# Five 64-token slots in the expert stage of a fused attention and mixture-of-experts kernel, their second layer with the weights stationary

## The reference

```python
x = x + xattn(layernorm(x), ctx)          # cosine similarity with a context, 256 wide
x = x + attention(layernorm(x))           # 16 heads of 16
x = x + ffn(layernorm(x))
# ffn: 14 experts, each token goes to one
logits = x @ router_w
assignments = argmax(logits); weights = softmax(logits)[assignments]
hid = gelu(x @ w1[e] + b1[e])             # 256 -> 512
out = (hid @ w2[e] + b2[e]) * weights     # 512 -> 256
```

## Time and profile before

| | |
|---|---|
| median of 3 runs | 495.64 us (494.65 to 496.19) |
| the profiled execution | 494.51 us |
| its span, first to last instruction | 492.7 us |
| TensorE busy | 479.8 us, 97% |
| TensorE weight loads busy | 384.0 us, 78% |
| granted TensorE clock | 1.000 |
| VectorE, ScalarE, GpSimd busy | 68%, 67%, 50% |

### The profile page before, as it was taken

One profiled execution on the slowest core, in us unless ns is written; L12 is line 12 of the kernel. 1 busy time (PEld: TensorE's weight loads), 2 busy tenths in 40 slices (PEclk: granted clock), 3 DMA queues, 4 the chain that ended last, 5 costly groups with the idle time before them and its releaser, 6 DMA issues.

```text
span 492.7 us, 13958 instructions
## 1 busy us (share of the span) xinstructions
PE 479.8 (97%) x4290; PEld 384.0 (78%) x4291; DVE 335.6 (68%) x1021; ACT 331.6 (67%) x804; POOL 243.9 (50%) x428
## 2 busy tenths in 40 slices
PE   8999999999999999999999999998999999999996
PEld 6544444567888888888888888877898999999995
DVE  3577665657788989999898999998573333333332
ACT  2765666569988998898898889886553334333432
POOL 3468764344444456474655657472555333233333
PEclk9999999999999999999999999999999999999999
DMA  8989997500001223313322221227465876675631
GB/s 305 284 195 298 297 311 207 177 2 2 1 2 39 51 88 98 98 61 87 100 57 91 67 59 51 67 84 227 152 220 160 266 229 203 207 232 192 193 131 37
DMA packets 35025, 69.32 MB, mean 141 GB/s; under 512 B 6592, under 2 KB 21826, under 8 KB 34960
## 3 DMA queue, kind: packets, MB, share of 16 engines
q1 hardware_dynamic: 31168, 59.40, 40.3%
q0 software_dynamic: 3360, 8.84, 4.8%
q10 hardware_dynamic: 432, 0.26, 0.2%
HBM read 57.61 MB, written 11.35 MB: 140 GB/s over the span
## 4 chain that ended last, share of the span: by engine, by line
PE 65%; DVE 6%; issue 4%; ACT 3%; POOL 2%; POOLq 0%; ACTq 0%; DVEq 0%
PE psum L1532 13%; PE psum L1545 12%; PE psum L1459 9%; PE psum L1436 6%; PE psum L1423 6%; PE psum L1415 6%; PE psum L1383 5%; PE psum L1488 5%; PE psum L1282 5%; DVE arena L912 1%; POOL tok L528 1%; POOL out L614 1%; ACT arena L1145 0%; DVE smax L901 0%; ACT arena L1181 0%
## 5 line engine op out<-in xcount | busy, mean ns | idle before, releaser
L1532 PEld LDWEIGHTS psum<-arena,ring 128*128 128x128 f32 x608 | 73.5, 192 | 2.6 <-issue 0.6
L1532 PE MATMUL psum<-arena,ring 128*128 128x128 f32 x608 | 74.1, 275 | 0.5 <-issue 0.5
L1545 PE MATMUL psum<-w_s,arena 128*128 x304 | 71.9, 380 | 0.0
L1215 ACT ACTIVATE arena<-psum 128x256 f32<-128x256 f32 x38 | 14.6, 385 | 81.7 <-PE psum L1282 74.8
L1036 DVE SCALAR_TENSOR_TENSOR arena<-psum,slot_rec,arena 128x256 f32<-128x256 f32 x38 | 18.4, 484 | 69.3 <-PE psum L1545 69.0
L556 POOL TENSOR_TENSOR ov<-o_n,v_s 128x256 f32<-128x256 f32 x32 | 26.1, 817 | 77.8 <-DVE o_n L794 77.8
L1545 PEld LDWEIGHTS psum<-w_s,arena 128*128 128x128 f32 x304 | 55.0, 190 | 6.1
L1181 ACT ACTIVATE arena<-kT,head_mask 128x256 f32<-128x256 f32 x128 | 59.3, 531 | 0.0
L614 POOL DMA_INDIRECT out<-arena,token_of x38 | 38.8, 1022 | 19.0 <-POOL token_of L606 14.1
L901 DVE TENSOR_REDUCE smax<-psum 128x16 f32<-128x1024 f32 x32 | 39.2, 1224 | 12.6 <-PE psum L1436 12.6
L1145 ACT ACTIVATE arena<-arena 128x1024 f32<-128x1024 f32 x32 | 33.8, 1057 | 19.0 <-DVE arena L912 18.9
(11 more groups left out here) (206 smaller groups left out, 1072.9 us busy)
## 6 DMA issues: line engine op xcount, KB each, us to landing
ring<-w SPq DMA_DIRECT2D x38, 512.0 KB
w_s<-ctxT SPq DMA_DIRECT2D x15, 768.0 KB, 8.5
w_s<-w SPq DMA_DIRECT2D x16, 448.0 KB, 3.4
slot_rec<-routed SPq DMA_DIRECT2D x38, 132.0 KB
tok<-x SPq DMA_DIRECT2D x16, 256.0 KB, 7.8
w_s<-xT SPq DMA_DIRECT2D x12, 256.0 KB, 6.8
routed<-pad_rec SPq DMA_DIRECT2D x1, 1980.0 KB, 8.6
tok<-b SPq DMA_DIRECT2D x14, 128.0 KB, 3.1
```

Of the source, the lines that this page charges most:

```text
L1532: mm = pe.matmul(hid_bank(p)[:, f * P:(f + 1) * P], w1_s[:, r, c * F + f * P:c * F + (f + 1) * P], xgT[:, p, c * P:(c + 1) * P], start=c = ...
L1545: mm = pe.matmul(bank(2 + q, D), hidT[:, q, f * P:(f + 1) * P], w2_s[:, bass.ds(e * (FC * D) + f * D, D)], start=f == 0, stop=f == FC - 1)
```

## The change

`EVEN` becomes 33 full slots, and five *half slots* of 64 tokens are put in at places 22, 25, 28, 31 and 34, so that 38 places are run always as before (`ALWAYS`), and 50 at most (`PLACES`). A half slot serves an expert whose token count leaves 64 or fewer over full slots. The steps are no longer a loop but written out.

In a half slot the records, the normalised tile, the moving operand of the first layer, the gelus and the rows of the output are 64 wide or long. The second layer is turned round: 128x128 blocks of w2 are stationary and 64 columns of the hidden values move, ScalarE copies the result from PSUM (`copy_turned`), and TensorE turns it back with two transposes (`turn_back`) one step later. Its w2 blocks come from DRAM in another order, five more loads of 512 KB by SyncE at slots 12, 14, 16, 18 and 20. The plan gets a second kind of count (`counts[:, 1]`, a subtraction, a maximum), and behind `plan_tables` two new pieces, `plan_halves` and `later_tables`.

```diff
+HALVES, HALF0, APART = 5, 22, 3
-EVEN = NTOK // P + E // 2 - 1
+EVEN = NTOK // P + 1
...
             def plan_counts():
-                plan(dve.tensor_scalar(counts[:, :], count, -1.0, None, ALU.add))
+                for n, short in enumerate((1, 1 + RG)):
+                    plan(dve.tensor_scalar(counts[:, n], count, -float(short), None, ALU.add))
...
+                plan(dve.tensor_tensor(ends[:, 0, 1, PAD0:], ends[:, 0, 1, PAD0:], ends[:, 0, 0, PAD0:], ALU.subtract))
+                settle()
+                at = sums_of(2)
+                plan(dve.scalar_tensor_tensor(ends[:, at, 0, PAD0:], ends[:, at, 1, PAD0:], -float(HALVES),
+                                              ends[:, at, 0, PAD0:], ALU.max, ALU.add))
+                settle()
...
+            def plan_halves(at):
+                plan(dve.scalar_tensor_tensor(half_from[:, 0:E], ends[0:1, at, 0, PAD0:], -float(P), origin[0:1, 0:E],
+                                              ALU.mult, ALU.add))
+                plan(dve.memset(half_from[:, E:E + 1], float(E * REGION - RG)))
+                plan(dve.scalar_tensor_tensor(passed_half[:, :, :],
+                                              ends[0:1, at, 1, PAD0:].unsqueeze(1).broadcast_to([1, HALVES, E]), -1.0,
+                                              slot_row[0:1, 0:HALVES].unsqueeze(2).broadcast_to([1, HALVES, E]),
+                                              ALU.mult, ALU.is_lt))
+                settle()
+                plan(dve.tensor_tensor(half_rise[:, :], half_from[:, 1:E + 1], half_from[:, 0:E], ALU.subtract))
+                plan(dve.tensor_reduce(expert_half[:, :], passed_half[:, :, :], AX.X, ALU.add))
+                settle()
+                plan(dve.tensor_tensor(risen_half[:, :, :], passed_half[:, :, :],
+                                       half_rise[:, :].unsqueeze(1).broadcast_to([1, HALVES, E]), ALU.mult))
+                plan(dve.tensor_scalar(expert_half[:, :], expert_half[:, :], float(E - 1), None, ALU.min))
+                settle()
+                plan(dve.tensor_reduce(base_half[:, :], risen_half[:, :, :], AX.X, ALU.add))
+                settle()
+                plan(dve.tensor_scalar(base_half[:, :], base_half[:, :], half_from[:, 0:1], float(RG), ALU.add, ALU.add))
+                settle()
+            def later_tables():
+                for n, (table, of_half) in enumerate(((expert_tab, expert_half), (base_tab, base_half))):
+                    spread = table[:, HALF0:HALF0 + APART * HALVES].rearrange("o (h r) -> o h r", r=APART)
+                    between = (APART - 1) * HALVES
+                    at = n * P + HALF0
+                    dve.tensor_copy(spread[:, :, 0], of_half[:, :]).then_inc(s["halves_ok"], 1)
+                    dve.tensor_copy(spread[:, :, 1:], bank(7)[0:1, at:at + between].rearrange("o (h r) -> o h r", r=APART - 1))\
+                        .then_inc(s["halves_ok"], 1)
+                    dve.tensor_copy(table[:, HALF0 + APART * HALVES:], bank(7)[0:1, at + between:n * P + NSLOT])\
+                        .then_inc(s["halves_ok"], 1)
...
             finish_slot(5, 5)
             plan_tables()
+            plan_halves(at)
+            later_tables()
...
+                if i == HEAD + 1:
+                    sp.wait_ge(s["halves_ok"], HALVES_TOLD)
+                n, odd = divmod(i - HEAD - 1, 2)
+                if 0 <= n < HALVES and not odd:
+                    of_half = sp.value_load(expert_tab[0:1, bass.ds(HALF0 + APART * n, 1)], min_val=0, max_val=E - 1)
+                    sp.dma_start(w2_half[:, n, :], w2e[bass.ds(of_half, 1)].rearrange("o p j -> (o p) j"))\
+                        .then_inc(s["w2_half_in"], 16)
...
+            def second_layer_turned(u, q):
...
+                for d in range(KC):
+                    for f in range(FC):
+                        mm = pe.matmul(bank(6)[:, d * RG:(d + 1) * RG], w2_half[:, n, f * D + d * P:f * D + (d + 1) * P],
+                                       hidT[:, q, f * P:f * P + RG], start=f == 0, stop=f == FC - 1)
...
+            def turn_back(u, q):
+                pe.wait_ge(s["g_yT"], halves_before(u) + 1)
+                need(pe, s["g_y"], u - 1)
+                turn(bank(2 + q, D), yT[:, :, :].rearrange("p d j -> p (d j)"), s["g_y_psum"])
...
-                t, u = i + 1, i - 1
+                t, u, v = i + 1, i - 1, i - 2
...
                 if within(i, part):
                     first_layer(i, k % 4)
+                if half(v):
+                    turn_back(v, (k - 2) % 2)
                 if within(t, part):
                     turn_slot(t, (k + 1) % 2)
+                if half(u):
+                    second_layer_turned(u, (k - 1) % 2)
+                elif within(u, part):
                     second_layer(u, (k - 1) % 2, e)
```

More of the change, by code:

```diff
@@ L35 @@
 NSLOT = NTOK // P + E - 1
-EVEN = NTOK // P + E // 2 - 1
+EVEN = NTOK // P + 1
+HALVES, HALF0, APART = 5, 22, 3
+HALVES_TOLD = 6
+ALWAYS = EVEN + HALVES
+PLACES = NSLOT + HALVES
 REGION = NTOK + P
@@ L55 @@
 RECS = 8
-LOOPED = HEAD + 1 + (EVEN - HEAD - 2) // RECS * RECS
 LOG_SCALE = 2.0 ** -10
@@ L97, in run_slots, with half, halves_before, width @@
 def run_slots(engine, step, first, last, used_tab, begin=0):
-    run_steps(engine, lambda i, k: step(i, k, (0, EVEN)), begin, EVEN + last, HEAD + 1, LOOPED, RECS)
+    for i in range(begin, ALWAYS + last):
+        step(i, i % RECS, (0, ALWAYS))
     used = engine.value_load(used_tab[0:1, 0:1], min_val=0, max_val=NSLOT)
     with engine.If(used > EVEN):
-        for i in range(EVEN + first, NSLOT + last):
-            step(i, i % RECS, (EVEN, NSLOT))
+        for i in range(ALWAYS + first, PLACES + last):
+            step(i, i % RECS, (ALWAYS, PLACES))
+def half(t):
+    return HALF0 <= t < HALF0 + APART * HALVES and (t - HALF0) % APART == 0
+def halves_before(t):
+    return sum(half(n) for n in range(t))
+def width(t):
+    return RG if half(t) else P
 def within(t, part):
@@ L1077, in _ @@
             plan_tables()
+            plan_halves(at)
+            later_tables()
             def expert_step(i, k, part):
-                t, u = i + 1, i - 1
+                t, u, v = i + 1, i - 1, i - 2
                 if within(t, part):
                     normalise_slot(t, (k + 1) % RECS)
-                if within(u, part):
+                if half(v):
+                    finish_slot(v, (k - 2) % RECS)
+                if within(u, part) and not half(u):
                     finish_slot(u, (k - 1) % RECS)
@@ L1261, in expert_step @@
                     act.wait_ge(s["plan_ok"], 3)
+                if i == HALF0:
+                    act.wait_ge(s["halves_ok"], HALVES_TOLD)
                 if within(i, part):
                     e = expert_of(i)
+                if half(i - 2):
+                    copy_turned(i - 2)
                 if within(t, part):
```

143 lines of the change are left out of this document (88 added, 55 removed).

## The result

The changed kernel takes 500.66 us (500.09 to 502.43, four runs) against 495.91 us of the kernel before. The ratio is 1.0097, with a 95% interval of 1.0066 to 1.0127. A second comparison, in the experiments, gave 1.0086 (1.0062 to 1.0111), +4.3 us. The change makes the kernel slower by 0.9%.

The account below looks back on a forecast made before the run. TensorE was taken to bound the expert stage, with VectorE's plan on the path between slots 5 and 7. Half slots +0.75, plan +0.6 and +1.8 made +3.15 us, 498.8 us on the median; range 495.8 to 501.0.

Parts of the forecast that it names:

- the prediction's own case: Whole kernel: half slots and both plan parts add +3.15 us, bounds 497.7 to 500.0 us; chance 0.60.
- The floor of a pair: TensorE, half slots: a pair with 128 weight columns costs what its load costs, 0.1075 us at 64 moving columns.
- The rival in which the moving columns set the pace: TensorE, half slots: 64 columns cost half, the change is -5.1 us, 490.5 us; chance 0.14.
- A half slot: TensorE: layers -0.06 and -0.01, `turn_back` +0.22, so +0.15 us each and +0.75 in five.
- The plan, part one: VectorE's list ahead of L1012: more instructions in `plan_counts`, TensorE already waiting, +0.6 us (0.5 to 0.7).
- The plan, part two: VectorE ahead of `normalise_slot(8)`: 2.2 us of new list, TensorE stands once for 1.8 us (1.3 to 2.3).
- the rival's paragraph: VectorE at slot 8: part two of the plan hidden or far cheaper, change +0 to +1.4 us; chance 0.16.
- No wait in the half slots: Half slots: ScalarE's copy of the turned result has 1.2 us of cover; narrower work on waiting engines saves nothing.
- The transfers: SyncE's queue, slots 12 to 21: five 512 KB loads stay covered at 276 GB/s on average, costed at 0.
- The rival of late transfers: Slots 12 to 21: w1 or records late, TensorE waits 1 to 2 us at two or three, about 503; chance 0.10.
- Writing the loop out: Expert loop: costs nothing, since steps ahead of the loop and inside it average 3.75 us.

Follow-up runs that it names:

- A second comparison: The changed kernel run once more with no edit, against the kernel before: 500.02 us, ratio 1.0086 (1.0062 to 1.0111).
- the 16-column run: Changed kernel with 16 instead of 64 moving columns in both layers of the half slots, 48 of 64 tokens left out: 499.93 us in one run.
- the narrower weights: Changed kernel with each half-slot weight block given as two of 64 columns: 495.51 us with the halves alternating, 501.57 us with the lower half first.
- Putting slot 8 first: Changed kernel with the normalisation of slot 8 moved ahead of the plan of the half slots: 497.89 us, ratio to the kernel before 1.0050.

## Why the prediction was right

It said slower, +3.15 us and 498.8 us, in a range of 495.8 to 501.0; the kernel took 500.66. The mechanism was right: weights that set the pace, and a plan on the path. The size was too small. +4.75 us is above the bounds of the prediction's own case (+2.05 to +4.35, 497.7 to 500.0 us), and 500.66 lies in the range only because that was widened for late transfers, which did not come. That part is luck; the second comparison, +4.3, is just within the bounds. Point by point:

- **The floor of a pair.** Said 0.1075 us for 64 columns between bounds of 0.1045 and 0.111; measured 0.108. The rival in which the moving columns set the pace is ruled out by the 16-column run, and the narrower weights show that the time goes with the stationary side. The reading came from twelve short records in another stage, and it held.
- **A half slot.** Said +0.15 with bounds of 0.05 and 0.27; measured +0.23. First layer -0.05 (said -0.06), turned layer 0.00 (said -0.01), transposes +0.22 (said the same). The rest, 0.06, is the full first layer behind the turned one, 1.84 instead of 1.78, which I had not listed.
- **The plan, part one.** Said +0.6; measured 0.35 to 0.5. The instructions cost what was said: from the start of `plan_counts` to `normalise_slot(7)` it is 2.31 us instead of 1.81, 1.70 and 1.70 in the three profiles of the kernel before. But in two of these the plan is ready within 0.1 us of the moment TensorE wants it, and the last wait ahead of the first layer of slot 7 is one for a gelu. "TensorE is already waiting there" was read from the one execution in which it did.
- **The plan, part two.** Said 2.2 us of list and 1.8 of stall; measured 2.26 (373.50 to 375.76) and 1.87 from first layer to first layer. The list is nine instructions and six copies, fifteen and not the ten that the rival's paragraph has; the sum had counted them all. Putting slot 8 first took away 2.1 us.
- **No wait in the half slots.** Said 1.2 us of cover for the copy; measured 1.36. VectorE and ScalarE wait for TensorE as before.
- **The transfers.** Said hidden, with 276 GB/s needed; the engines moved 320 to 345 at a share of 0.95 to 0.97, and TensorE had no gap. The rival of late transfers did not happen, and taking the five loads out gained nothing, but there was little room left.
- **Writing the loop out.** Said zero, and this is the weak step of the sum. I checked it where TensorE runs, and there it holds, but not at the end of the kernel: with the loop alone written out the last scatter lands 0.5 and 1.8 us later. In time it measured +1.3 us (0.2 to 2.5), of which a lower clock accounts for most.

The sum as measured: 0.35 to 0.5 + 1.87 + 5 x 0.23 is 3.4 to 3.5 us on TensorE's path. With about 1.2 of the end (3.7 against 2.5) it is 4.6 to 4.7 us, within the intervals of both comparisons (+4.3 and +4.8). The path is shown by experiments; that the rest is the landing, and in no part the start, is only argued.

**What stays open.** Why the last scatter lands later when code far ahead of it is written out. The issue and the last stretch of code are the same. In the 4 us behind the last issue there are two transfers of one instruction queue in all ten profiles with written-out steps, and one in the three of the kernel before. In three of the ten (landings of 4.15, 4.3 and 4.6 us) two single packets come about a microsecond behind the others. But late packets are not all of it: in the first profile of the changed kernel (4.15) and the second of the written-out loop (3.0) the last packet moves 2.0 to 2.1 us behind the issue, as in the kernel before, and only the wait ends later. Whether the fetch causes the delay was not tried.

## What to carry to other kernels

Before making the moving side of a product narrower, find the product in the trace that has the same stationary width and the fewest moving columns: if its start-to-start time is near that of the full one, the moving side does not set the pace, and narrowing it gains next to nothing. In fp32 with 128 stationary columns that was so from 128 moving columns down to 16 (0.111 to 0.107 us); two 64-column blocks to alternate halves of PSUM's partitions got below it. And new bookkeeping on a serial engine goes behind the work that the next engine is waiting for: 2.3 us of list cost 1.9 us or nothing, by its place alone.

## What the runs showed of the hardware that I had not expected

- With fp32 data, a load and matmul pair with 128 stationary columns takes 0.111, 0.108 and 0.107 us for 128, 64 and 16 moving columns.
- Pairs with 64 stationary and 64 moving columns take 0.057 us in one column half, and 0.034 to 0.037 where products to the two halves alternate.
- Going from 128 to 64 stationary columns costs about 0.09 us ahead of the first such pair, and 0.05 to 0.11 in what follows the last one.
- Eight pairs with 64 stationary columns against 256 moving ones take 1.87 us, where 128 stationary columns take 1.73: the narrower load went with the slower layer.
- With a loop written out in the middle of the kernel and nothing else changed, the last scatter landed in 4.3 and 3.0 us, where it took 2.4 to 2.5 with the loop.
